# Moving the scores and the down projection within a slot of a six-layer local-attention kernel

## The reference, cut to what matters

```python
# attention: 16 heads of 64, windows of 32 tokens, each sees itself and the window before
qkv = shift_tokens(x) @ Wqkv
q, k = l2norm(q) * qs, l2norm(k) * ksc     # then rotary tables
sim = einsum(q, k of own and previous window) * 8, masked
x = x + softmax(sim) @ v @ Wo
# feed-forward, 341 inner channels
hg = layernorm(shift_tokens(x)) @ W1 + b1
a, gate = split(hg)
x = x + (a * gelu(gate)) @ W2 + b2
```

## Time and profile before

| | |
|---|---|
| Median of 3 runs | 1733.32 us (1729.53 to 1735.44) |
| Span of the profiled execution | 1731.0 us (its own time is not shown apart) |
| TensorE busy | 95%, 25970 matmuls |
| VectorE, ScalarE, GpSimd busy | 84%, 82%, 76% |
| Mean granted clock of TensorE | 0.986 of full speed |

### The profile page before, as it was taken

One profiled execution on the slowest core, in us unless ns is written; L12 is line 12 of the kernel. 1 busy time (PEld: TensorE's weight loads), 2 busy tenths in 40 slices (PEclk: granted clock), 3 DMA queues, 4 the chain that ended last, 5 costly groups with the idle time before them and its releaser, 6 DMA issues.

```text
span 1731.0 us, 68758 instructions
## 1 busy us (share of the span) xinstructions
PE 1639.0 (95%) x25970; PEld 1277.2 (74%) x25970; DVE 1446.3 (84%) x3011; ACT 1425.6 (82%) x2851; POOL 1311.9 (76%) x1305
## 2 busy tenths in 40 slices
PE   7779999999999999999999999999999999999995
PEld 5657777777777777777777777777777777777773
DVE  4499888888888888888888888888888888888884
ACT  3367888888888888888888888888888888888885
POOL 6088877877877787787778778787877877777765
PEclk9799999999999999999999999999999999999997
DMA  4111111111111111111111111111111101111000
GB/s 140 41 38 43 35 33 36 30 48 38 41 32 30 36 36 42 49 30 32 30 36 42 49 36 30 32 30 48 38 41 36 30 27 38 35 30 32 28 24 26
DMA packets 41426, 66.40 MB, mean 38 GB/s; under 512 B 7072, under 2 KB 16032, under 8 KB 41376
## 3 DMA queue, kind: packets, MB, share of 16 engines
q1 hardware_dynamic: 40224, 65.38, 12.7%
q10 hardware_dynamic: 1152, 0.34, 0.1%
HBM read 20.61 MB, written 1.05 MB: 13 GB/s over the span
## 4 chain that ended last, share of the span: by engine, by line
PE 61%; ACT 28%; issue 6%; DVE 4%; ACTq 1%; DMA 0%; POOL 0%; DVEq 0%; POOLq 0%
PE ps_qs L530 12%; PE ps_po L530 9%; PE ps_q L530 8%; PE ps_a L530 7%; PE ps_tk L530 7%; PE ps_f L530 6%; PE ps_po L650 5%; ACT p_bd L943 4%; PE ps_k L530 4%; PE ps_v L530 4%; ACT squares L949 4%; ACT L1053 3%; ACT L1050 3%; ACT q_t L943 3%; ACT prob L987 2%
## 5 line engine op out<-in xcount | busy, mean ns | idle before, releaser
L427 POOL TENSOR_TENSOR qk<-qk,rnorm 128x512 f32<-128x512 f32 x384 | 393.6, 1046 | 176.6 <-DVE rnorm L1284 176.1
L419 POOL TENSOR_TENSOR qk<-qk,qk_rot 128x512 f32<-128x512 f32 x384 | 483.8, 1282 | 0.0
L434 POOL TENSOR_TENSOR prob<-prob,row_inv 128x512 f32<-128x512 f32 x192 | 200.7, 1045 | 92.8 <-DVE row_inv L1301 92.8
L1289 DVE TENSOR_REDUCE row_max<-ps_qs 128x8 f32<-128x512 f32 x191 | 132.0, 691 | 164.8 <-PE ps_qs L530 164.8
L943 ACT COPY p_bd<-ps_po 64x512 f32<-64x512 f32 x378 | 219.1, 580 | 58.8 <-PE ps_po L650 56.4
L1264 DVE TENSOR_REDUCE ssq<-squares 128x8 f32<-128x512 f32 x384 | 261.4, 681 | 3.4 <-ACT squares L949 3.4
L530 PEld LDWEIGHTS ps_qs<-k_t,q_t 64*32 64x32 f32 x12224 | 179.2, 107 | 69.0 <-issue 68.9
L943 ACT COPY attn_t<-ps_po 128x512 f32<-128x512 f32 x191 | 112.5, 589 | 133.2 <-PE ps_po L530 133.1
L530 PE MATMUL ps_qs<-k_t,q_t 64*32 64x64 f32 x12224 | 210.1, 218 | 0.0
L530 PE MATMUL ps_po<-p_bd,v_back 128*64 128x64 f32 x3056 | 193.2, 225 | 0.0
L530 PEld LDWEIGHTS ps_po<-p_bd,v_back 128*64 128x64 f32 x3056 | 163.1, 137 | 35.8 <-issue 17.0
(11 more groups left out here) (237 smaller groups left out, 4082.7 us busy)
## 6 DMA issues: line engine op xcount, KB each, us to landing
v_back<-v_own SPq DMA_DIRECT2D x192, 192.0 KB, 2.4
w_raw<-in_wqkv SPq DMA_DIRECT2D x48, 192.0 KB, 2.4
v_back<-v_own SPq DMA_DIRECT2D x96, 64.0 KB, 2.1
wo_sb<-in_wo SPq DMA_DIRECT2D x12, 256.0 KB, 2.9
w_sb<-in_w SPq DMA_DIRECT2D x6, 341.0 KB, 3.1
w_sb<-in_w SPq DMA_DIRECT2D x6, 192.0 KB, 2.7
x_in<-in_x SPq DMA_DIRECT2D x4, 256.0 KB, 4.2
out<-s_out SPq DMA_DIRECT2D x8, 128.0 KB, 1.9
```

Source lines behind the costliest of these rows:

```text
L419: nc.gpsimd.tensor_tensor(qk[:, s, i, :], qk[:, s, i, :], qk_rot[:, s, i, :], ALU.add).then_inc(added, 1)
L427: nc.gpsimd.tensor_tensor(heads(qk[:, s, i, :]), heads(qk[:, s, i, :]), rnorm[:, s, 8 * i:8 * i + 8].unsqueeze(2).to_broadcast([P, 8, HEAD ...
L434: nc.gpsimd.tensor_tensor(heads(prob[:, s, :]), heads(prob[:, s, :]), row_inv[:, s, :].unsqueeze(2).to_broadcast([P, 8, HEAD]), ALU.mult). ...
L1289: V.tensor_reduce(row_max[:, s, :], heads(ps[:]), AX, ALU.max).then_inc(max_done, 1)
```

## The change

The scores are no longer issued between the q projection and the turn of p for unit u-3, but at the end of the slot, behind the value matmuls, for unit u-2. The drain loses the scores that it began with. The down projection of iteration n-4 goes from slot 1 to slot 2, behind the second up projection and ahead of the values; the wait on `x_ready` ahead of the key turn and VectorE's residual addition go from slot 2 to slot 3 with it. In slot 0 the spread of the layer norm's factors is issued ahead of the half out projection. ScalarE's, GpSimd's and SP's lists are not changed.

```diff
@@ TensorE, body
                     project(n, j, 0, ps_q, q_scaled, q_done)
-                    if live(u - 3):
-                        scores(u - 3, (j - 3) % UNITS, (j - 3) % 2)
                     if live(u - 4):
                         turn_p(u - 4, j % 2)
...
                     if live(u - 2):
                         turn_qk(u - 2, 0, j % 2)
-                        if j == 2 and live_batch(n - 4):
+                        if j == 3 and live_batch(n - 4):
                             pe.wait_ge(x_ready, BATCHES + n - 3)
                         turn_qk(u - 2, 1, j % 2)
                     if j == 0:
+                        if live_batch(n - 3):
+                            ln_spread(n - 3, u)
                         if live_batch(n - 2):
                             out_projection(n - 2, 1)
-                        if live_batch(n - 3):
-                            ln_spread(n - 3, u)
                     if j == 1:
...
-                        if live_batch(n - 4):
-                            ff_down(u - 2, n - 4)
                     if j == 2:
...
+                        if live_batch(n - 4):
+                            ff_down(u - 2, n - 4)
...
                     if live(u - 4):
                         values(u - 4, n - 1, j, j % 2)
+                    if live(u - 2):
+                        scores(u - 2, (j - 2) % UNITS, j % 2)
@@ TensorE, drain
-                scores(b, 1, 1)
                 turn_p(a, 0)
```

## The result

| | before | after |
|---|---|---|
| Median | 1733.98 us (4 runs, 1729.53 to 1735.44) | 1765.66 us (4 runs, 1762.15 to 1771.05) |
| Ratio | | 1.0187, 95% interval 1.0158 to 1.0215 |
| Span of the profiled execution | 1731.0 us | 1767.2 us |
| TensorE, ScalarE busy | 95%, 82% | 91%, 80% |

The change makes the kernel 32 us slower; 44 were forecast, with a range of 1746 to 1798.

The account below looks back on a forecast made before the run. TensorE was taken as the bound (95% busy), with ScalarE late in slot 1. Four slots summed to 34.64 us against 33.63, +1.0 an iteration; 44 iterations added 44 us to 1733.3, giving 1777 us, range 1746 to 1798.

Parts of the forecast that it names:

- The slots: Loop iteration, each slot counted from scores to scores: 8.31, 8.44, 9.33 and 8.56 us, 34.64 in all against 33.63 before.
- The two waits: Scores wait 1.32 us for ScalarE's mask in slot 1; down projection waits 0.88 us for the key copy in slot 2.
- The spread at nothing: Slot 0, layer norm's spread ahead of the half out projection: zero, bounds 0 and +0.3 us an iteration.
- The loop's jump: End of slot 3 into slot 0: no term of its own; slot 3 was put at 8.64 - 0.08 = 8.56 us.
- The transitions: Gaps between TensorE's matmul groups where the scores moved: 0.08 us a slot saved, bounds 0 and 0.15.
- ScalarE's chain: From squares of q: 6.20 us to the mask in slot 1, 4.70 to the key copy in slot 2, 0.19 to TensorE.
- 44 iterations times the difference: Loop iterations with a down projection: +1.0 us each makes +44 us; first four iterations and drain left as they are.
- The rivals: Three other outcomes: both waits vanish (4%), the wait only moves (1729 us, 8%), a third wait joins (12%).
- Neither wait vanished: Slots 1 and 2: rival that both waits vanish and TensorE alone sets 32.44 us an iteration, 1681 us; chance 4%.
- neither slot 0 nor slot 3 waits for ScalarE: Rival that slots 0 and 3 wait too, or late engines pass delay on: some 0.5 us an iteration, 1799 us; chance 12%.
- the turn of q gets cover: Turn of q's wait for VectorE's subtraction: distance from the scores' start, 2.93 us, becomes 0.82 longer.
- The rule on weight loads: Scores' first load would hide behind the values: up to 4 x 0.08 x 44 = 14 us, giving 1763 us.

## Why the prediction was right, and where it was off

*What bounds the kernel.* Right: TensorE, with ScalarE late in slot 1. The run with the down projection behind the values shows it from the other side, since covering that wait alone gives back the 0.9 us.

*The slots.* Forecast and measured, from scores to scores:

| slot | forecast | measured | of it waiting |
|---|---|---|---|
| 0 | 8.31 | 8.44 | 0.48 idle behind the jump |
| 1 | 8.44 | 8.47 | 1.38 (forecast 1.32) |
| 2 | 9.33 | 9.17 | 0.77 (forecast 0.88) |
| 3 | 8.56 | 8.32 | none |
| sum | 34.64 | 34.40 | |

The two waits were right in place, in releaser and, to 0.11 us, in size. The terms that were off:

- *The spread at nothing.* It saves 0.34 us where TensorE sets the slot, as in slot 0 here. The prediction asked only whether its input was there in time, not where its weight load falls. The bounds of 0 to +0.3 had the wrong sign.
- *The loop's jump.* With the values ahead of it the q projection came 0.17 us later than behind other values (the prediction left this in slot 3). With the scores ahead, in slot 0, it comes 0.55 later: 885.02 - 883.44 = 1.58, where the next slot has 892.91 - 891.88 = 1.03. That is 0.38 us more, and the spread's 0.34 nearly cancel it. That the sum came out so near is in part luck.
- *The transitions.* The prediction took 0.08 us a slot. Slot 3 went from 8.64 to 8.32 us; 0.17 of this is the jump's gap gone from it, so 0.15 is left. The other 0.07 is the turn of p to the k projection, 0.35 (885.82 to 886.17 in the trace) from 0.41.
- *ScalarE's chain.* In slot 2 it was 0.14 us shorter than forecast, 4.56 from squares to key copy. In slot 1 it was as forecast, but from the mask's end to the scores 0.26 us passed, not 0.19.

*44 iterations times the difference.* 0.72 us in the median iteration make the 32 measured; 1.0 us and 44 were forecast. The direction and both mechanisms stand. The size is 12 us too large, and the terms above make 11 of them (34.64 - 34.40, times 44).

*The rivals.* Neither wait vanished, and neither slot 0 nor slot 3 waits for ScalarE. What the prediction did not have as a rival is VectorE. The sum said that the turn of q gets cover, and in the changed kernel it does. But seven of the kernels above have the down projection in slot 2 and wait less for ScalarE than the changed one. In six of them the turn of q waits 0.2 to 0.6 us for VectorE. With the down projection in slot 1 behind the values TensorE waits for neither.

*The rule on weight loads.* The Trainium skill, *TensorE: Matmul & The Clock Gate*, in its section on a matmul's steps, has loads pulled ahead of running matmuls when the row groups do not conflict or the load goes to the background weight buffer. The runs show both: the spread's load behind the key turn is pulled ahead, and behind the out projection it is not. Which of the two conditions decided there, no row shows. For the scores behind the values the prediction worked out 1763 us by this rule, near the 1765.66 measured, but not by that way. In the changed kernel the scores' first load stands as in the drain, at the same 891.88 as their first matmul:

```profile
891.61 0.20 PEld L530 LDWEIGHTS ps_po<-p_bd,v_own 128*64 128x64 f32 x4
891.88 0.49 PEld L530 LDWEIGHTS ps_qs<-k_t,q_t 64*32 64x32 f32 x32
```

## What to carry to other kernels

Where an instruction waits for a late engine, first look for independent work behind it on its own queue and put the waiting one behind that: here the values' 1.04 us covered a wait of 0.87, for 40 us. Moved to another slot it still asks for that slot's input: the wait was 0.19 us there with the scores in their old place, for a gain of 22 us, and 0.76 with the scores at the slot's end. Before you pull a consumer to the end of a slot, add up the cycle through the other engine from both ends: the consumer also stands ahead of what that engine waits for next. And an order that saves time on one engine is worth nothing until that engine sets the pace of its slot, so try such edits again when another wait has gone. When a wait grows, read the granted clock too: with a wait of 1.90 us an iteration some iterations ran partly at the lower clock.

## What was not expected of the hardware

- TensorE's gap at the loop's jump depends on what runs ahead of it: 0.17 us beyond the usual with the values (128x64 matmuls) in front, 0.50 to 0.55 us (0.43 to 0.48 of it idle) with the scores' 64 small matmuls, 16 ns apart. That it was the jump with the scores ahead is shown by the run that took one slot's scores back; why, is open.
- A weight load is begun early behind some matmuls and not behind others: 0.39 us without a load in one order of the spread and the out projection, none in the other, with the same two groups and no dependence between them. In the loops of the kernels before and after there is a pattern. Where the weights of two neighbouring groups are both wider than 64 columns, or both 64 columns wide, the first load of the second group starts 0.03 to 0.24 us ahead of its matmul in the median (the groups behind a wait left aside). Where the width changes between these two, or to or from the scores' 64x32, load and matmul start within 0.01 us of each other. Behind the same out projection, in the changed kernel, the values' first load starts 0.22 us early:

```profile
890.64 0.36 PEld L530 LDWEIGHTS ps_po<-p_bd,v_back 128*64 128x64 f32 x4
890.86 0.28 PE L530 MATMUL ps_po<-p_bd,v_back 128*64 128x64 f32 x4
```

  The old order of slot 0 changes width between key turn, out projection, spread and values three times, the new one once. That this is where the 0.34 us come from is argued from the traces; no run changes a width alone.
